# A two-layer transformer kernel: GpSimd's weight subtractions cut into 256-column pieces, and layer 0's gate operations spread over more places

## The chip, the cores and the metric

The kernel runs on one core of a Trainium2 chip. The metric is the device time of one execution in microseconds (us).

## What is computed

Input x has 4 batches of 1024 tokens with 128 features. Layer 0 adds to x a multi-query attention and a "SwitchHead" attention, both on the normalised x; layer 1 does the like with a linear attention and a mixture of experts. The change touches the SwitchHead part of layer 0 (8 heads, 8 experts each, 128 wide):

```python
raw = einsum('bsd,ed->bse', x, w).reshape(B, S, H, E)
probs = sigmoid(raw)
vals, idx = top_k(probs, 2)
vals = vals / clip(vals.sum(-1, keepdims=True), 1e-09) * route_scale
gate = (one_hot(idx, E) * vals[..., None]).sum(-2)      # for gate_v and for gate_o
xv = einsum('bsd,hedp->bshep', x, v_w)
v = einsum('bshep,bshe->bhsp', xv, gate_v)
att = softmax(einsum('bhqp,bhkp->bhqk', q, k) * SCALE)
ctx = einsum('bhqk,bhkp->bqhp', att, v)
out = einsum('bshep,hepd->bsd', ctx[:, :, :, None, :] * gate_o[..., None], o_w)
```

## The kernel before, in words

Layer 0 is the function `layer0`. It handles 32 steps (`N0`), one for each batch and SwitchHead head; in each step two heads of the multi-query attention are done beside it. Every engine has a block of its own in which one loop over `i` lists, by hand, what the engine does in which order; an engine does its list strictly in order, and semaphores join the lists. A tile is 128 tokens; there are 8 per batch. PSUM has a ring of five 512-column tiles, `ring`, and a two-bank tile, `wide`. TensorE takes the next ring tile with `claim`, which waits until the reader of the tile's last content is done. So a late VectorE operation that reads a ring tile holds up the matmuls five claims further on.

What matters of one step:

- **TensorE**: `values` (x times the value weights of 8 experts, 1024 columns per tile, as L79, L80 and L81), `peak_scores` (L254) and `scores_by_key` (L329) for the other attention, `scores` (into `wide`), `turn` (L295, transposes of the probabilities), `weigh` (L307), `outputs` (L79 to L81 with the output weights), `turn_peaks` (L274, needs L1139 of VectorE), `sum_by_key` (L344).
- **VectorE**: `take_peaks` (L1114) and `find_largest` (L1157) are maxima over PSUM tiles; `gate_values` (L1127) and `gate_outputs` (L1187) multiply a ring tile by the gates into `vprod` and `oprod`; `output_gates` (L1167 and L1169) works on small SBUF tiles; `cut_peaks` (L1137 to L1139), then `shift_queries` (L1146), which `scores` of tile 0 needs; `split_queries` (L65, L1106); `lower_ctx`. Between these stand eight calls `batch_work(i - 1, place)`, places 0 to 7.
- **GpSimd**: `sum_values` (L774 to L776) adds the experts' halves of `vprod` down to one tile of `vs`, `sum_outputs` (L783 to L787) those of `oprod` and adds them to x. Once per step it runs `lower_wv` and `lower_wo`.
- **ScalarE**: exponentials, copies out of PSUM, and the upper halves of the weights.

**Weight halves.** For precision each 32-bit operand is split in an upper part, rounded by the copy to the matmul's type, and a lower part, the difference. The weights of one head are 128 x 1024. They come by DMA into `wraw`, ScalarE copies the upper half (L826 and L834), and GpSimd's helper `lower` (L69) subtracts: one instruction of 1024 columns for the value weights (`m_wvs`), one for the output weights (`m_wos`). In GpSimd's order `lower_wv` stands between `sum_outputs` of tiles 3 and 4, and `lower_wo` between `sum_values` of tile 1 and of tile 2. TensorE's `values(i, 0, 0)` and the load of the next output weights wait for `wv_ready`; `outputs(n, 0, 0)` and the load of value weights wait for `wo_ready`.

**Batch work.** Per batch some work is left that belongs to no head: normalising, gates, keys, queries. VectorE does it for the batch after the current one in the `batch_work` calls; `s = i % 8` names the head of the batch, and `place` the call. The gates (`gates(b, part)`) are 16 parts for tiles 0 to 3 (q = 0) and the same 16 for tiles 4 to 7 (q = 1). One part is one link of a chain in which each operation waits for the one before (`gs` does that). Parts 0 to 12 find the two largest of 8 experts and take reciprocals. Part 13 is five operations on 64 or 128 columns (L1283 to L1287): the sum of the two inverses, the maximum with 1e-9, its reciprocal, the route scale, and the product. Part 14 (L1290, L1291) multiplies both choices by their shares, part 15 (L1293) adds them. Where the parts stand:

```python
                    if s == 1 and place >= 5:
                        gates(after, place - 5)
                    if s == 2 and place not in (0, 4):
                        gates(after, 2 + place - place // 4)
                    if s == 3 and place:
                        gates(after, 8 + place)
                    if s in (4, 5):
                        gates(after, 16 + 8 * (s - 4) + place)
```

So q = 0 ends in s = 3 (part 13 at place 5, part 14 at place 6, part 15 at place 7), and q = 1 in s = 5, at the same places; s = 4 has L1272 (part 6 of q = 1) at place 6. In s = 6 there are no gates. `lower_keys` (L1249) shares place 5 in s = 2 and s = 3, and `normalise` and `normalise_out` (L1214, L1225) stand at places 4 to 7 of s = 7 and s = 0. `choose_experts`, the routing of layer 1, ends with L1343; once it is called at s = 0, place 1. Place 1 lies between `cut_peaks` and `shift_queries`, place 5 before `gate_outputs` of tile 6, place 6 between the maxima of tile 3. For batch 0 all parts run in a row before the loop.

Of the kernel before, what the change touches and what calls it, by code (L numbers as in the profile page):

```python
# [31 lines left out]
def spread(ap, n):  # L32

    return ap.unsqueeze(len(ap.shape)).to_broadcast([*ap.shape, n])
# [33 lines left out]
def lower(eng, lo, src, hi):  # L68
    return eng.tensor_tensor(lo.bitcast(F32R), src, hi, ALU.subtract)  # L69
# [79 lines left out]
def layer0(nc, whole, a, x, xnT, ident, order, combine):  # L149
# [4 lines left out]
    with ExitStack() as ctx:  # L154
# [23 lines left out]
        wraw = m.sbuf("wraw", [D, ES * PS])  # L178
        wvs, wos = m.sbuf("wvs", [D, 2, ES * PS]), m.sbuf("wos", [PS, 2, ES * D])
# [20 lines left out]
        x_upper, wv_upper, wo_upper, x_ready, wv_ready, wo_ready, qk_upper, qk_ready, zeroed, zeros_stored, q_stored = m.sems(  # L200
            "x_upper wv_upper wo_upper x_ready wv_ready wo_ready qk_upper qk_ready zeroed zeros_stored q_stored")
# [23 lines left out]
        with nc.Block() as block:  # L225
# [483 lines left out]
            def _(pool):  # L709
# [46 lines left out]
                def lower_wv(n):  # L756
                    if n not in steps:
                        return
                    pool.wait_ge(wv_upper, n + 1)
                    lower(pool, wvs[:, 1, :], wraw[:, :], wvs[:, 0, :]).then_inc(wv_ready, 1)  # L760

                def lower_wo(n):
                    if n not in steps:
                        return
                    pool.wait_ge(wo_upper, n + 1)
                    lower(pool, wos[:, 1, :], wraw[:, :], wos[:, 0, :]).then_inc(wo_ready, 1)

                def sum_values(n, t):
                    if n not in steps:
# [326 lines left out]
            def _(v):  # L1096
# [155 lines left out]
                def gates(b, part):  # L1252
                    if b not in batches:
                        return
                    q, part = part // 16, part % 16
                    flat = gate_of[b % 2][:, 4 * q:4 * q + 4, :].rearrange("p t (g e) -> p (t g) e", e=ES)
                    ranks = order[:, :].unsqueeze(1).to_broadcast([P, 64, ES])
                    if part == 0:
                        v.wait_ge(gates_exp, 4 * b + 2 * q + 2)
                        gs(v.scalar_tensor_tensor(out=g_v[:, :, :], in0=flat, scalar=1.0, in1=flat, op0=ALU.add, op1=ALU.max))  # L1260
                    if part == 1:
                        gs(v.tensor_reduce(g_pair[:, 0, :], g_v[:, :, :], AX.X, ALU.min))
                    if part == 2:
                        gs(v.tensor_tensor(g_c[:, :, :], g_v[:, :, :], spread(g_pair[:, 0, :], ES), ALU.is_equal))
                    if part in (3, 9):
                        gs(v.tensor_tensor(g_c[:, :, :], g_c[:, :, :], ranks, ALU.mult))
                    if part in (4, 10):
                        gs(v.tensor_reduce(g_m[:, :], g_c[:, :, :], AX.X, ALU.max))
                    if part == 5:
                        gs(v.tensor_tensor(g_one[:, :, :], g_c[:, :, :], spread(g_m[:, :], ES), ALU.is_equal))  # L1270
                    if part == 6:
                        gs(v.scalar_tensor_tensor(out=g_v[:, :, :], in0=g_one[:, :, :], scalar=3.0e38, in1=g_v[:, :, :],  # L1272
                                                  op0=ALU.mult, op1=ALU.add))
                    if part == 7:
                        gs(v.tensor_reduce(g_pair[:, 1, :], g_v[:, :, :], AX.X, ALU.min))
                    if part == 8:
                        gs(v.tensor_tensor(g_c[:, :, :], g_v[:, :, :], spread(g_pair[:, 1, :], ES), ALU.is_equal))
                    if part == 11:
                        gs(v.tensor_tensor(g_other[:, :, :], g_c[:, :, :], spread(g_m[:, :], ES), ALU.is_equal))
                    if part == 12:  # L1280
                        gs(v.reciprocal(g_inv[:, :, :], g_pair[:, :, :]))
                    if part == 13:
                        gs(v.tensor_tensor(g_m[:, :], g_inv[:, 0, :], g_inv[:, 1, :], ALU.add))  # L1283
                        gs(v.tensor_tensor(g_m[:, :], g_m[:, :], tiny[:, :].to_broadcast([P, 64]), ALU.max))
                        gs(v.reciprocal(g_m[:, :], g_m[:, :]))
                        gs(v.tensor_tensor(g_m[:, :], g_m[:, :], route[:, :].to_broadcast([P, 64]), ALU.mult))
                        gs(v.tensor_tensor(g_inv[:, :, :], g_inv[:, :, :], g_m[:, :].unsqueeze(1).to_broadcast([P, 2, 64]),  # L1287
                                           ALU.mult))
                    if part == 14:
                        v.tensor_tensor(g_one[:, :, :], g_one[:, :, :], spread(g_inv[:, 0, :], ES), ALU.mult)  # L1290
                        gs(v.tensor_tensor(g_other[:, :, :], g_other[:, :, :], spread(g_inv[:, 1, :], ES), ALU.mult))  # L1291
                    if part == 15:
                        v.tensor_tensor(flat, g_one[:, :, :], g_other[:, :, :], ALU.add).then_inc(gates_ready, 1)  # L1293
                        v.wait_ge(gates_ready, 2 * b + q + 1)

# [59 lines left out]
                def batch_work(i, place):  # L1355
                    if i not in steps:
                        return
                    s, after, before, early = i % HS, i // HS + 1, i // HS - 1, i // HS - 2
                    if s in (1, 2) and place in (0, 4):
                        keep_v32(after, 2 * s - 2 + place // 4)  # L1360
                    if s in (2, 3) and place == 5:
                        lower_keys(after, s - 2)
                    if s == 0 and place == 2:
                        invert_dens(before)
                    if s == 4 and place in (0, 4):
                        add_attn(before, place // 4)
# [3 lines that stand above are left out]
                        gates(after, 2 + place - place // 4)  # L1370
                    if s == 3 and place:
                        gates(after, 8 + place)
                    if s in (4, 5):
                        gates(after, 16 + 8 * (s - 4) + place)
                    if s == 7 and place >= 4:
                        normalise(after + 1, (place - 4) // 2, place % 2)
                    if before == B - 2:
                        if s == 5 and place < 4:
                            token_moments(before, place)
                        if s == 5 and place == 4:  # L1380
                            statistics_out(before)
                        if s == 6 and place == 3:
                            rstd_out(before)
                        if s == 6 and place >= 4:
                            normalise_out(before, place // 6, place % 2)
                    elif s == 7 and place < 4:
                        token_moments(before, place)
                    if early < B - 2:
                        if s == 0 and place == 0:
                            statistics_out(early)  # L1390
                        if s == 0 and place == 5:
                            rstd_out(early)
                        if s == 0 and place >= 6:
                            normalise_out(early, 0, place % 2)
                        if s == 1 and place in (2, 3):
                            normalise_out(early, 1, place % 2)
                        if s == 3 and place == 4:
                            keep_routing(early)
                    if early == 1:
                        if s == 0 and place == 1:  # L1400
                            choose_experts(early - 1)
                        if s == 1 and place == 7:
                            mix(early - 1)
                        if s == 6 and place == 7:
                            choose_experts(early)
                        if s == 7 and place == 5:
                            mix(early)
# [18 lines left out]
                for q in range(2):  # L1426
                    normalise(1, q, 0)
                    normalise(1, q, 1)
                for part in range(32):
                    gates(0, part)  # L1430
                for i in range(-1, N0 + 1):
                    take_peaks(i, 5, 0, 1)
# [850 lines left out]
```

## Time and profile before

| what | value |
|---|---|
| median of 3 runs (lowest, highest) | 3594.96 us (3593.2, 3598.66) |
| the profiled execution: its own time, its span | 3593.13 us, 3591.4 us |
| mean granted TensorE clock | 0.967 |
| TensorE's matmuls busy | 3299.4 us (92%) |
| VectorE busy | 2363.4 us (66%) |
| GpSimd busy | 1755.3 us (49%) |
| the 32 + 32 subtractions (L69, 1024 columns) | 76.6 + 76.2 us, mean 2392 and 2382 ns |

The span runs from the first to the last instruction of the profiled execution; its own time is 1.7 us longer. In the names PE is TensorE, DVE VectorE, ACT ScalarE and POOL GpSimd. `m_wvs`, `m_wos` and so on are the tiles of the code with a prefix. A clock of 1.00 is 2.4 GHz, and 0.50 is 1.2 GHz.

### The profile page before, as it was taken

The page shows a single profiled execution, that of the slowest core. Times are in us where ns is not written, and L with a number is a line of the kernel's source. Part 1 is how long each engine was busy: PE and PEld are TensorE (multiplying, and loading weights), DVE is VectorE, ACT ScalarE, POOL GpSimd, SP SyncE. Part 2 cuts the span into 40 slices and gives each one's busy share as a digit, 9 for nine tenths or more (in the row PEclk, how much of TensorE's full clock was granted, in tenths as well). Part 3 has the DMA queues.
Part 4 walks back from the last instruction along what each step waited for, and adds up shares of the span by engine and source line. Part 5 has one row for each costly group of instructions (what it writes and reads, how often), then busy time and mean ns, then how long its engine had stood idle before and what let it go on. Part 6 is the DMA issues. An engine that isn't in the chain of part 4 may idle for free. (4 is left out here: it accounts for less than half of the span.)

```text
span 3591.4 us, 53232 instructions
## 1 busy us (share of the span) xinstructions
PE 3299.4 (92%) x19284; PEld 2311.3 (64%) x19284; DVE 2363.4 (66%) x3586; ACT 1687.0 (47%) x2854; POOL 1755.3 (49%) x1986
## 2 busy tenths in 40 slices
PE   3899999999999999999999999999993799989897
PEld 2566666666666666666666666666662677777675
DVE  6777888787888888888888888877863212122221
ACT  1445544545554445555454544555551363534444
POOL 1466656566665566666566665665652212121111
PEclk6999999999999999999999999999996899999998
DMA  3000000001000110010000001100003000000000
GB/s 86 18 25 26 19 19 28 28 26 31 20 19 19 30 33 25 20 32 19 24 29 28 19 20 32 31 19 19 25 2 67 9 1 1 1 1 1 1 1 24
DMA packets 115927, 79.23 MB, mean 22 GB/s; under 512 B 28618, under 2 KB 104020, under 8 KB 115668
## 3 DMA queue, kind: packets, MB, share of 16 engines
q1 hardware_dynamic: 113364, 73.46, 7.6%
q10 hardware_dynamic: 2304, 2.36, 0.3%
q8 instruction: 157, 2.57, 0.3%
q14 instruction: 102, 0.84, 0.1%
HBM read 63.74 MB, written 12.06 MB: 21 GB/s over the span
## 5 line engine op out<-in xcount | busy, mean ns | idle before, releaser
L883 ACT ACTIVATE m_expA<-m_ring 128x512 f32<-128x512 f32 x1024 | 547.5, 602 | 420.5 <-PE m_ring L329 297.4
L1114 DVE TENSOR_REDUCE m_peaks<-m_ring 128x1 f32<-128x512 f32 x1024 | 653.0, 684 | 126.1 <-PE m_ring L254 119.0
L774 POOL TENSOR_TENSOR m_vprod<-m_vprod 128x512 f32<-128x512 f32 x256 | 333.5, 1303 | 622.0 <-DVE m_vprod L1127 620.7
L783 POOL TENSOR_TENSOR m_oprod<-m_oprod 128x512 f32<-128x512 f32 x256 | 327.8, 1280 | 328.5 <-DVE m_oprod L1187 328.2
L307 PE MATMUL m_ring<-m_probT,m_vs 128*128 128x256 f32 x2048 | 466.8, 381 | 1.7 <-ACT m_probT L864 1.7
L864 ACT ACTIVATE m_probT<-m_ring 128x512 f32<-128x512 f32 x512 | 284.3, 601 | 363.5 <-PE m_ring L295 333.8
L307 PEld LDWEIGHTS m_ring<-m_probT,m_vs 128*128 128x128 f32 x2048 | 391.2, 191 | 60.3 <-ACT m_probT L864 2.2
L1127 DVE TENSOR_TENSOR m_vprod<-m_ring,m_gate 128x512 f32<-128x512 f32 x512 | 341.4, 687 | 77.7 <-POOL m_vs L776 55.0
L1157 DVE TENSOR_REDUCE m_neg<-m_wide 128x1 f32<-128x1024 f32 x256 | 312.7, 1221 | 105.7 <-PE m_wide L81 105.4
L1187 DVE TENSOR_TENSOR m_oprod<-m_ring,m_go 128x512 f32<-128x512 f32 x512 | 347.0, 688 | 31.0 <-PE m_ring L81 16.5
L2161 POOL TENSOR_TENSOR k_x<-k_x,m_mixed 128x512 f32<-128x512 f32 x72 | 91.9, 1276 | 534.5 <-DVE m_mixed L1970 534.5
L2080 ACT ACTIVATE m_hT<-m_ring,l_b 128x512 f32<-128x512 f32 x288 | 182.7, 686 | 352.5 <-PE m_ring L81 352.3
L1970 DVE TENSOR_TENSOR m_mixed<-m_ring,k_combine 128x512 f32<-128x512 f32 x72 | 49.8, 692 | 450.7 <-PE m_ring L1810 450.7
L854 ACT ACTIVATE m_prob<-m_wide,m_neg 128x1024 f32<-128x1024 f32 x256 | 288.3, 1126 | 104.3 <-DVE m_neg L1157 104.3
L295 PE MATMUL m_ring<-k_ident,m_prob 128*128 128x128 f32 x2048 | 275.9, 277 | 26.9 <-DVE m_peaks L1114 26.1
L295 PEld LDWEIGHTS m_ring<-k_ident,m_prob 128*128 128x128 f32 x2048 | 233.0, 142 | 92.8 <-issue 66.3
L1810 PEld LDWEIGHTS m_ring<-l_w,m_hT 128*128 128x128 f32 x2304 | 273.6, 195 | 8.9 <-issue 2.7
L344 PE MATMUL m_sums<-m_expA,m_v 128*32 128x512 f32 x2048 | 275.1, 609 | 1.5 <-ACT m_expA L883 1.4
L1810 PE MATMUL m_ring<-l_w,m_hT 128*128 128x128 f32 x2304 | 274.2, 278 | 1.1 <-ACT m_qpT L2060 1.1
L79 PE MATMUL m_ring<-m_wvs,m_xs 128*128 128x512 f32 x512 | 237.2, 463 | 35.1 <-DVE m_oprod L1187 23.6
L254 PE MATMUL m_ring<-m_ks,m_qs 32*128 32x512 f32 x1024 | 229.4, 504 | 33.4 <-DVE m_qs L1106 28.5
L79 PE MATMUL m_wide<-m_xs,m_yT 128*128 128x512 f32 x512 | 231.0, 451 | 9.2 <-DVE m_qs L1146 5.7
(249 smaller groups left out, 6239.5 us busy)
## 6 DMA issues: line engine op xcount, KB each, us to landing
m_wraw<-in_v_w SPq DMA_DIRECT2D x32, 512.0 KB, 4.0
m_qf<-q_dram SPq DMA_DIRECT2D x128, 128.0 KB, 2.7
m_wraw<-in_o_w SPq DMA_DIRECT2D x32, 512.0 KB, 3.8
q_dram<-m_kf SPq DMA_DIRECT2D x24, 256.0 KB, 4.3
sums_dram<-m_sumsT ACTq DMA_DIRECT2D x128, 18.0 KB
m_o_in<-sums_dram SPq DMA_DIRECT2D x64, 32.0 KB
m_rden_in<-rden_dram SPq DMA_DIRECT2D x64, 32.0 KB
p_w<-in_w SPq DMA_DIRECT2D x1, 2048.0 KB, 8.3
```

Source lines behind the costliest of these rows:

```text
L79: pe.matmul(out, wh, xh, start=True, stop=False)
L295: last = pe.transpose(ps[:, c * P:(c + 1) * P], prob[t % 2][:, (4 * h + c) * P:(4 * h + c + 1) * P], ident[:, :])
L307: last = pe.matmul(ps[:, 0:2 * P], vs[n % 2][:, k, :], probT[g % 2][:, k, :], start=(k == 0), stop=(k == TPB - 1))
L774: vchain(pool.tensor_tensor(vprod[:, 0:512], vprod[:, 0:512], vprod[:, 512:1024], ALU.add))
L783: ochain(pool.tensor_tensor(op[:, 0:512], op[:, 0:512], op[:, 512:1024], ALU.add))
L854: act.activation(prob[t % 2][:, :], wide.home["scores", n, t][:, :], ACT.Exp, bias=neg[t % 2][:, :], accum_out=den[n % 2][:, t:t + 1]).the ...
L883: act.activation(expA[hh][:, c * 512:(c + 1) * 512], ring.home["scT", n, k, hh, c][:, :], ACT.Exp)\
L1114: v.tensor_reduce(peaks[:, t, hh, c:c + 1], ring.home["peaks", n, t, hh, c][:, :], AX.X, ALU.max)\
L1127: v.tensor_tensor(vprod[:, c * 512:(c + 1) * 512].rearrange("p (e d) -> p e d", e=4), ring.home["values", n, t, c][:, :].rearrange("p (e d ...
L1157: v.tensor_reduce(neg[t % 2][:, :], wide.home["scores", n, t][:, :], AX.X, ALU.max, negate=True)\
L1187: v.tensor_tensor(oprod[t % 2][:, c * 512:(c + 1) * 512].rearrange("p (e d) -> p e d", e=4), ring.home["outputs", n, t, c][:, :].rearrange ...
L1810: last = pe.matmul(ps[:, t * P:(t + 1) * P], hT[j % 2][:, k, t * P:(t + 1) * P], w2[:, e, k, :], start=(k == 0), stop=(k == HT - 1))
```

## The change

GpSimd's two subtractions per step become four instructions of 256 columns each; the semaphore is raised by the last. The five operations of part 13 become four parts (13: the sum; 14: the maximum; 15: reciprocal and route scale; 16: the product), so that q = 0 and q = 1 have 19 parts each, 38 together; six of them now stand in s = 6. In s = 3 places 5, 6 and 7 hold parts 13, 14 and 15; s = 4 begins with parts 16, 17, 18 of q = 0 and goes on with parts 0 to 4 of q = 1; s = 5 has parts 5 to 12 of q = 1, and s = 6 has parts 13 to 18 at places 0 to 5.

```diff
--- before.py
+++ after.py
@@ -757,13 +757,17 @@
                     if n not in steps:
                         return
                     pool.wait_ge(wv_upper, n + 1)
-                    lower(pool, wvs[:, 1, :], wraw[:, :], wvs[:, 0, :]).then_inc(wv_ready, 1)
+                    for cols in (slice(256 * k, 256 * (k + 1)) for k in range(4)):
+                        last = lower(pool, wvs[:, 1, cols], wraw[:, cols], wvs[:, 0, cols])
+                    last.then_inc(wv_ready, 1)
 
                 def lower_wo(n):
                     if n not in steps:
                         return
                     pool.wait_ge(wo_upper, n + 1)
-                    lower(pool, wos[:, 1, :], wraw[:, :], wos[:, 0, :]).then_inc(wo_ready, 1)
+                    for cols in (slice(256 * k, 256 * (k + 1)) for k in range(4)):
+                        last = lower(pool, wos[:, 1, cols], wraw[:, cols], wos[:, 0, cols])
+                    last.then_inc(wo_ready, 1)
 
                 def sum_values(n, t):
                     if n not in steps:
@@ -1252,7 +1256,7 @@
                 def gates(b, part):
                     if b not in batches:
                         return
-                    q, part = part // 16, part % 16
+                    q, part = part // 19, part % 19
                     flat = gate_of[b % 2][:, 4 * q:4 * q + 4, :].rearrange("p t (g e) -> p (t g) e", e=ES)
                     ranks = order[:, :].unsqueeze(1).to_broadcast([P, 64, ES])
                     if part == 0:
@@ -1281,15 +1285,18 @@
                         gs(v.reciprocal(g_inv[:, :, :], g_pair[:, :, :]))
                     if part == 13:
                         gs(v.tensor_tensor(g_m[:, :], g_inv[:, 0, :], g_inv[:, 1, :], ALU.add))
+                    if part == 14:
                         gs(v.tensor_tensor(g_m[:, :], g_m[:, :], tiny[:, :].to_broadcast([P, 64]), ALU.max))
+                    if part == 15:
                         gs(v.reciprocal(g_m[:, :], g_m[:, :]))
                         gs(v.tensor_tensor(g_m[:, :], g_m[:, :], route[:, :].to_broadcast([P, 64]), ALU.mult))
+                    if part == 16:
                         gs(v.tensor_tensor(g_inv[:, :, :], g_inv[:, :, :], g_m[:, :].unsqueeze(1).to_broadcast([P, 2, 64]),
                                            ALU.mult))
-                    if part == 14:
+                    if part == 17:
                         v.tensor_tensor(g_one[:, :, :], g_one[:, :, :], spread(g_inv[:, 0, :], ES), ALU.mult)
                         gs(v.tensor_tensor(g_other[:, :, :], g_other[:, :, :], spread(g_inv[:, 1, :], ES), ALU.mult))
-                    if part == 15:
+                    if part == 18:
                         v.tensor_tensor(flat, g_one[:, :, :], g_other[:, :, :], ALU.add).then_inc(gates_ready, 1)
                         v.wait_ge(gates_ready, 2 * b + q + 1)
 
@@ -1370,7 +1377,7 @@
                         gates(after, 2 + place - place // 4)
                     if s == 3 and place:
                         gates(after, 8 + place)
-                    if s in (4, 5):
+                    if s in (4, 5) or s == 6 and place < 6:
                         gates(after, 16 + 8 * (s - 4) + place)
                     if s == 7 and place >= 4:
                         normalise(after + 1, (place - 4) // 2, place % 2)
@@ -1426,7 +1433,7 @@
                 for q in range(2):
                     normalise(1, q, 0)
                     normalise(1, q, 1)
-                for part in range(32):
+                for part in range(38):
                     gates(0, part)
                 for i in range(-1, N0 + 1):
                     take_peaks(i, 5, 0, 1)
```

The order of instructions shows the moves. First VectorE in s = 3 around place 5, before: L1187 is `gate_outputs`, L1249 `lower_keys`, `m_g_...` are the gates' tiles.

```order
L1187 TENSOR_TENSOR m_oprod<-m_ring,m_go 128x512
L1249 SCALAR_TENSOR_TENSOR m_ks<-m_ks,m_split,m_kf 128x512
L1283 TENSOR_TENSOR m_g_m<-m_g_inv 128x64
L1284 TENSOR_TENSOR m_g_m<-m_g_m,m_tiny 128x64
L1285 RECIPROCAL m_g_m<-m_g_m 128x64
L1286 TENSOR_TENSOR m_g_m<-m_g_m,m_route 128x64
L1287 TENSOR_TENSOR m_g_inv<-m_g_inv,m_g_m 128x128
L1187 TENSOR_TENSOR m_oprod<-m_ring,m_go 128x512
L1157 TENSOR_REDUCE m_neg<-m_wide 128x1
```

And with the change (line numbers are four higher up to the sum of the inverses, L1287, and up to seven higher behind it):

```order
L1191 TENSOR_TENSOR m_oprod<-m_ring,m_go 128x512
L1253 SCALAR_TENSOR_TENSOR m_ks<-m_ks,m_split,m_kf 128x512
L1287 TENSOR_TENSOR m_g_m<-m_g_inv 128x64
L1191 TENSOR_TENSOR m_oprod<-m_ring,m_go 128x512
L1161 TENSOR_REDUCE m_neg<-m_wide 128x1
L1131 TENSOR_TENSOR m_vprod<-m_ring,m_gate 128x512 x2
```

Four operations have left the place between L1249 and the next `gate_outputs`. Then VectorE in s = 3, places 6 and 7, before:

```order
L1114 TENSOR_REDUCE m_peaks<-m_ring 128x1 x3
L1290 TENSOR_TENSOR m_g_one<-m_g_one,m_g_inv 128x512
L1291 TENSOR_TENSOR m_g_other<-m_g_other,m_g_inv 128x512
L1114 TENSOR_REDUCE m_peaks<-m_ring 128x1
L1127 TENSOR_TENSOR m_vprod<-m_ring,m_gate 128x512 x2
L1157 TENSOR_REDUCE m_neg<-m_wide 128x1
L1293 TENSOR_TENSOR m_gate<-m_g_one,m_g_other 128x512
L1127 TENSOR_TENSOR m_vprod<-m_ring,m_gate 128x512
```

And with the change:

```order
L1118 TENSOR_REDUCE m_peaks<-m_ring 128x1 x3
L1289 TENSOR_TENSOR m_g_m<-m_g_m,m_tiny 128x64
L1118 TENSOR_REDUCE m_peaks<-m_ring 128x1
L1131 TENSOR_TENSOR m_vprod<-m_ring,m_gate 128x512 x2
L1161 TENSOR_REDUCE m_neg<-m_wide 128x1
L1291 RECIPROCAL m_g_m<-m_g_m 128x64
L1292 TENSOR_TENSOR m_g_m<-m_g_m,m_route 128x64
L1131 TENSOR_TENSOR m_vprod<-m_ring,m_gate 128x512
```

The two products of 512 columns have left place 6, which now holds one operation on 64 columns; place 7 holds a reciprocal and a product on 64 columns in place of the last addition. The products now stand in s = 4, at place 1. Last, GpSimd around the output weights, before:

```order
L774 TENSOR_TENSOR m_vprod<-m_vprod 128x512
L775 TENSOR_TENSOR m_vprod<-m_vprod 128x256
L776 TENSOR_TENSOR m_vs<-m_vprod 128x128
L69 TENSOR_TENSOR m_wos<-m_wraw,m_wos 128x1024
L774 TENSOR_TENSOR m_vprod<-m_vprod 128x512
```

And with the change:

```order
L778 TENSOR_TENSOR m_vprod<-m_vprod 128x512
L779 TENSOR_TENSOR m_vprod<-m_vprod 128x256
L780 TENSOR_TENSOR m_vs<-m_vprod 128x128
L69 TENSOR_TENSOR m_wos<-m_wraw,m_wos 128x256 x4
L778 TENSOR_TENSOR m_vprod<-m_vprod 128x512
```

Nothing has moved against its neighbours there; the one subtraction is now four in a row.

## Rows read from the trace of the kernel before

**Rows 1.** The page, part 1: busy us, share of the span, instructions of each engine.

```profile
PE 3299.4 (92%) x19284; PEld 2311.3 (64%) x19284; DVE 2363.4 (66%) x3586; ACT 1687.0 (47%) x2854; POOL 1755.3 (49%) x1986
```

**Rows 2.** TensorE's waits, 100 to 2640 us: us in total, times, longest.

```profile
PE m_ring L295 <- DVE m_peaks L1114: 26.1, 13, 2.5
PE m_ring L79 <- DVE m_oprod L1187: 23.6, 13, 4.3
...
PE m_wide L79 <- DVE m_qs L1146: 5.7, 1, 5.7
```

**Rows 3.** Windows: length; PE, PEld, DVE, ACT, POOL busy (x); PEclk; DMA share; GB/s.

```profile
1004.47:1086.91 82.44, 80.82 (x426) 54.47 (x425) 68.00 (x101) 41.50 (x75) 52.88 (x61) 1.00 0.07 21
1086.91:1177.82 90.91, 82.76 (x426) 55.02 (x425) 74.57 (x105) 42.18 (x75) 49.86 (x60) 0.94 0.07 19
...
1261.37:1343.90 82.53, 78.07 (x410) 52.41 (x409) 67.34 (x100) 40.17 (x73) 49.77 (x59) 0.98 0.10 30
...
2484.44:2562.79 78.35, 77.61 (x416) 52.22 (x415) 63.59 (x99) 39.74 (x72) 48.83 (x59) 1.00 0.08 22
```

**Rows 4.** Timeline of TensorE, phases 3, 3, 4, 5 and 7: start, us, operation [idle before].

```profile
1105.01 0.76 PE L79 MATMUL m_ring<-m_wvs,m_xs 128*128 128x512 f32 x1 [4.26 <-DVE m_oprod L1187]
...
1132.83 1.06 PE L295 MATMUL m_ring<-k_ident,m_prob 128*128 128x128 f32 x8 [2.45 <-DVE m_peaks L1114]
...
1217.88 1.06 PE L295 MATMUL m_ring<-k_ident,m_prob 128*128 128x128 f32 x8 [1.84 <-DVE m_peaks L1114]
...
1275.46 0.47 PE L79 MATMUL m_ring<-m_wvs,m_xs 128*128 128x512 f32 x1 [1.79 <-DVE m_oprod L1187]
...
1461.04 1.06 PE L295 MATMUL m_ring<-k_ident,m_prob 128*128 128x128 f32 x8 [1.51 <-DVE m_peaks L1114]
```

**Rows 5.** Timeline of VectorE, same columns, single operations.

```profile
58.84 0.23 DVE L1284 TENSOR_TENSOR m_g_m<-m_g_m,m_tiny 128x64 f32<-128x64 f32 x1
...
1017.06 0.88 DVE L1249 SCALAR_TENSOR_TENSOR m_ks<-m_ks,m_split,m_kf 128x512 fp32r<-128x512 f32 x1
...
1087.00 2.30 DVE L1169 TENSOR_TENSOR m_go<-m_gate,m_rden 128x16 f32<-128x16 f32 x1
...
1099.42 1.30 DVE L1283 TENSOR_TENSOR m_g_m<-m_g_inv 128x64 f32<-128x64 f32 x1
...
1103.30 0.83 DVE L1287 TENSOR_TENSOR m_g_inv<-m_g_inv,m_g_m 128x128 f32<-128x128 f32 x1
...
1128.96 2.40 DVE L1290 TENSOR_TENSOR m_g_one<-m_g_one,m_g_inv 128x512 f32<-128x512 f32 x1
...
1214.62 2.38 DVE L1272 SCALAR_TENSOR_TENSOR m_g_v<-m_g_one,m_g_v 128x512 f32<-128x512 f32 x1
...
1425.07 0.60 DVE L1214 TENSOR_SCALAR m_xn<-k_x,m_mean,m_rstd 128x128 f32<-128x128 f32 x2
...
1458.12 2.17 DVE L1214 TENSOR_SCALAR m_xn<-k_x,m_mean,m_rstd 128x128 f32<-128x128 f32 x2
...
2159.43 2.31 DVE L1343 TENSOR_TENSOR m_lg<-m_lg,m_t_first 128x64 f32<-128x64 f32 x1
```

**Rows 6.** Timeline of GpSimd, single operations.

```profile
1016.93 0.46 POOL L787 TENSOR_TENSOR k_x<-k_x,m_oprod 128x128 f32<-128x128 f32 x1
...
1017.36 1.72 POOL L774 TENSOR_TENSOR m_vprod<-m_vprod 128x512 f32<-128x512 f32 x1
...
1022.07 0.73 POOL L784 TENSOR_TENSOR m_oprod<-m_oprod 128x256 f32<-128x256 f32 x1
...
1023.83 1.28 POOL L774 TENSOR_TENSOR m_vprod<-m_vprod 128x512 f32<-128x512 f32 x1
...
1128.43 2.38 POOL L69 TENSOR_TENSOR m_wos<-m_wraw,m_wos 128x1024 fp32r<-128x1024 f32 x1
```

**Rows 7.** Timeline of VectorE in a head without batch work.

```profile
2602.95 0.69 DVE L1127 TENSOR_TENSOR m_vprod<-m_ring,m_gate 128x512 f32<-128x512 f32 x1 [1.68 <-POOL m_vs L776]
...
2605.18 0.42 DVE L69 TENSOR_TENSOR m_ctxT<-m_ring,m_ctxT 128x256 fp32r<-128x256 f32 x1 [1.07 <-ACT m_ctxT L874]
```

## Prediction, made before the changed kernel ran

> **What bounds the kernel now.** Start with the busy shares: TensorE works 92% of the span, VectorE 66%, GpSimd 49% [rows 1]. So only what makes TensorE stand, or slows its clock, can change the time. Next, TensorE's waits from 100 to 2640 us, which is layer 0 without its ends: the first two lines, with VectorE as the releaser, make 50 us, and one single wait for L1146 5.7 us [rows 2]. Then the windows, cut where GpSimd starts the subtraction for the value weights of one head after another [rows 3]. "Phase s" is from here on the batch work's number at that start; its places 3 to 7 lie in the window, and places 0 to 2 of the next phase at its end. The last row is a head without batch work: 78.35 us, TensorE busy 77.61. Phases 2, 3 and 5 take 82.44, 90.91 and 82.53. Phase 3 records as many matmuls as phase 2 (426) and is 8.5 us longer: idle time grows from 1.62 to 8.15 us, and busy time from 80.82 to 82.76, with the granted clock at 0.94 instead of 1.00. The timeline of TensorE shows where the idle time sits [rows 4]: 4.26 and 2.45 us in phase 3, 1.84 in phase 4, 1.79 in phase 5 (and a second 2.45 there), 1.51 in phase 7. The pattern stands three times, once for each later batch; the 1.51 kind stands at four heads.
>
> VectorE's timeline names the causes [rows 5]. The 4.26 us wait ends behind five small gate operations, the first at 1099.42, the last ended at 1104.13. The waits before L295 end behind L1290 and L1291, L1272, or two L1214. L1290 takes 2.40, L1272 2.38, the two L1214 2.17 together, though the same two take 0.60 elsewhere. Set GpSimd beside it [rows 6]: its subtraction for the output weights starts at 1128.43 and takes 2.38 us; L1290 starts 0.53 us later and ends 0.55 us after it. So a VectorE operation with two SBUF sources, and L1214 with one, doesn't get through before the GpSimd instruction then under way has ended.
>
> **The gates' operations in four places.** In phase 3, place 5, four of the five leave. From the end of the first (1100.72) to the end of the last (1104.13) that is 3.41 us, all in front of the L1187 that frees a ring tile for TensorE: 4.26 falls to 0.85. In phase 5 place 5 holds one 512-wide reduction instead (about 0.6 us, near the 0.55 that L1290 needs once it runs), and 1.79 falls to 0. Nobody but VectorE's own queue waits for these operations: the gates are read a batch later.
>
> The later parts move back three places, in the second half of a batch six. Place 6 gets: in phase 3 one 64-wide operation (0.23 us, from the uncontended row of L1284) for L1290 and L1291; in phase 4 the product with the ranks for L1272; in phase 5 L1279 for L1290 and L1291. New are two products at place 1 of phase 4, ahead of L1146, and six parts in phase 6, which had none. Between turning the peaks and the scores that need L1146 TensorE has the values of tile 7 and a transpose, and in phase 4 a projection and the queries too. So the products may cost nothing; at most 4.8, if each lasts as L1290 does. I take 0.5, nearer the cover. Phase 6 gets the five operations (4.7 us at phase 3's contended durations) and three 512-wide ones (1.8): at most 6.5, at least 0. They stand one or two to a place, where the other phases hold as much and TensorE shows no wait over 1 us, so I take 1.0.
>
> **The subtractions in pieces.** A 256-column GpSimd operation takes 0.73 us, a 512-column one 1.28 [rows 6]. Four pieces are 2.92 us against 2.38: 0.54 us more for each of 64 subtractions, 35 us of GpSimd's time. Who waits for that? For the value weights nobody soon: their reader stands half a head later in TensorE's order. Behind the output weights stands the sum of tile 2's values, for which VectorE waits 1.68 us in a head without batch work; and then, two small operations later, 1.07 us for ScalarE [rows 7]. A sum that is 0.54 us late disappears in that 1.07, so I price it at nothing; were that cover gone, it would be 0.54 x 32 = 17 us.
> The Trainium skill, page "GPSIMD Engine Reference", section "Elementwise — side-by-side cycle accounting", gives a two-input operation about 2.6 cycles an element at 1.2 GHz, and no price for one instruction more. By that alone four pieces last as long as one whole; the rows disagree, with 0.73 for 256 columns where half of 1.28 is 0.64, and the sum goes by the rows.
>
> What a piece gives: an operation that starts 0.53 us into the subtraction waits until the first piece ends, 0.2 us instead of 1.85. How much of VectorE's delay at place 6 reaches TensorE can be read off: L1272 2.4 us of delay, 1.84 of wait; L1290 with L1291 3.0 and 2.45; two L1214 2.1 and 1.51. The cover is 0.6 us each time. So at place 6:
> - phase 3: delay 0.2 + 0.23, the wait of 2.45 goes to 0
> - phases 4 and 5: 0.2 + 0.6, the waits of 1.84 and 2.45 go to 0.2
> - normalising (four heads): 0.2 + 0.3, then the second L1214 meets the second piece, 0.73 + 0.3; together 1.5, and 1.51 goes to 0.9.
> At the value weights L1169 takes 2.30 us at worst and should stay under 0.9; VectorE idles soon after, so I book nothing. In the head with the 5.7 us wait the routing's last operation, L1343, is 2.31 us of it; with pieces about 0.9, so 1.4 saved.
>
> Does the port change hands between two pieces? One place bears on it: L1249 starts at 1017.06, inside L787; L787 ends at 1017.39; the next GpSimd operation, listed from 1017.36 with no wait, takes 1.72 us instead of 1.28, as if it had begun when L1249 ended [rows 5, 6]. VectorE got in between two adjacent GpSimd instructions. I take that as how it goes.
>
> **The sum.** Per batch, three times: phase 3 saves 3.41 + 2.45, and 1.94 by the clock (82.76 - 80.82): 7.8. Phase 4 saves 1.6. Phase 5 saves 1.79 + 2.2 and 1.0 by the clock (0.98 over 82.53 us is 3.3 us at the lower level, 1.6 lost, of which I take two thirds): 5.0. That is 14.4 x 3 = 43.2. Normalising 0.6 x 4 = 2.4; routing 1.4, and 0.5 for the clock. Together 47.5. Against it phase 6 with 1.0 x 3, phase 4's products 0.5 x 3, and 2 for small new waits: 6.5. Net 41. From the profiled execution's 3593.1 us that is 3552; the median of the runs shown is 1.8 us higher, so 3554.
>
> **Rivals.**
> B. GpSimd keeps the port through its four adjacent pieces, since they wait for nothing. For it: each piece is ready when the last ends. Against it: the place of L1249. Then the pieces change only the length. Phase 3 keeps 3.4, 0.5 and 1.2 of clock; phase 4 loses 0.6; phase 5 keeps 1.8 and 0.6 of clock: 6.9 x 3 = 20.7, less 0.5 x 5 for normalising and routing and the 6.5. About 12 saved: 3583.
> The Trainium skill, page "SBUF — State Buffer", section "SBUF: two separate sides", calls the pair of ports that VectorE shares with GpSimd an exclusive lock, held for the whole instruction by whoever starts first; by that rule a queued piece could start first each time. On "whole instruction" the trace agrees (L1290 ends 0.55 us after the 2.38 us subtraction); on who is next it has the place of L1249.
> C. The waits go, but a part comes back: VectorE loses the pauses in which it caught up, and ring tiles are freed late elsewhere. For it: TensorE idles 0.74 us even in a head without batch work, so it is never far ahead or behind. With a third of the 47.5 returning 25 us are saved: 3570.
> D. Slower. Short GpSimd instructions cost more here than in the chains, and the sum of tile 2 is late in every head. It decides from the point where the subtraction's excess uses up the 1.07 and the 0.6 of cover, at pieces of (2.38 + 1.67) / 4 = 1.01 us. At 1.28 each, the 512-column duration, the excess is 2.74 - 1.67 = 1.07 us x 32 = 34 us, and such pieces give back most of place 6; with 12 us kept, 3617. Against it: 0.73 for that width.
>
> **How the numbers follow.** Forecast 0.70 (3543 to 3566), B 0.13, C 0.12, D 0.03, and 0.02 for gains and new waits that cancel. A measurement of this kernel tells 0.2%, some 7 us, from no change. All but D and the last are faster by more: 0.95, 0.02, 0.03. The likeliest gives 3554. The range goes up through C to 3575 and down to 3543, where the work added to phases 4 and 6 costs nothing and every clock loss goes.
>
> **What would show it.** Pieces near 0.73 us; in phase 3 the new place 6 (the maximum with the small constant) under 0.5 us; a wait near 0.9 where 4.26 stood, without a lower clock behind it; waits before the probability transposes under 1 us; phase 3 near 83 us, phase 5 near 79. Wrong would be: two-source operations that still last over 2 us inside a subtraction (B), VectorE waiting over 2.7 us for the sum of tile 2 (D), or new waits of over 1 us in phases 4 and 6 (C).

## The result, and the profile after

| | before | changed |
|---|---|---|
| median of 6 runs (lowest, highest) | 3596.41 us (3593.2, 3599.15) | 3539.9 us (3537.73, 3541.45) |
| ratio to before, 95% interval | | 0.9842 (0.983 to 0.9855) |
| span of the profiled execution | 3591.4 us | 3537.4 us |

The changed kernel is 56.5 us faster, 1.6%; the spans differ by 54.0 us. The forecast was 41 us and 3554; the time lies 3 us under the range. The direction and the places are right, several sizes are not. In the experiments below one run each of choice and both took 9654.92 and 4143.19 us, for which nothing here gives a cause, and the ratios leave these two out.

The list of TensorE's waits from 100 to 2640 us of the changed kernel (us in total, times, longest), against [rows 2]:

```profile
PE m_ring L79 <- DVE m_oprod L1191: 7.9, 10, 1.3
PE m_wide L79 <- DVE m_qs L1150: 4.1, 1, 4.1
...
PE m_ring L295 <- DVE m_peaks L1118: 2.6, 10, 0.4
```

The waits before L295 fell from 26.1 to 2.6 us, those of L79 for `gate_outputs` from 23.6 to 7.9. Together that is 39 us. The rest is mostly busy time. From the second window's start to the last one's, before and changed:

```profile
118.28:2562.79 2444.51, 2371.94 (x12576) 1595.87 (x12576) 1985.04 (x2968) 1222.95 (x2209) 1490.28 (x1740) 0.99 0.09 25
...
119.12:2510.42 2391.30, 2359.30 (x12575) 1589.47 (x12575) 1949.47 (x2968) 1219.32 (x2209) 1524.40 (x1919) 1.00 0.09 25
```

TensorE's idle time there falls from 72.6 to 32.0 us, and its busy time by 12.6 for the same matmuls, while the mean granted clock rises from 0.99 to 1.00. The windows by step, cut as before (length; busy us of PE, PEld, DVE, ACT, POOL; granted clock), phases 2, 3, 5 and 6, and the head with the long routing:

```profile
986.38:1068.86 82.48, 80.84 (x426) 54.49 (x425) 68.53 (x101) 41.41 (x75) 53.65 (x67) 1.00 0.07 21
1068.86:1148.63 79.77, 78.68 (x426) 53.09 (x425) 67.82 (x102) 41.87 (x75) 51.86 (x65) 1.00 0.08 22
...
1230.73:1308.33 77.60, 76.92 (x412) 51.45 (x411) 64.90 (x101) 40.33 (x73) 51.12 (x65) 1.00 0.11 32
1308.33:1387.21 78.88, 77.85 (x416) 52.49 (x415) 65.11 (x102) 39.65 (x72) 50.61 (x64) 1.00 0.08 22
...
2108.93:2195.32 86.39, 83.05 (x426) 56.38 (x427) 68.73 (x108) 43.28 (x77) 49.68 (x64) 0.96 0.14 33
```

Phase 2 is unchanged. Phase 3 fell from 90.91 to 79.77 [rows 3]; its idle time from 8.15 to 1.09, and its busy time from 82.76 to 78.68. That is lower than phase 2's 80.84 at the same count of matmuls and the same clock: the two windows hold different matmuls. Phase 5 fell from 82.53 to 77.60.

The timelines of the changed kernel, one row of TensorE, two of VectorE, and GpSimd's four pieces, show why:

```profile
1082.56 0.47 PE L79 MATMUL m_ring<-m_wvs,m_xs 128*128 128x512 f32 x1 [0.83 <-DVE m_oprod L1191]
```

```profile
1080.39 1.30 DVE L1287 TENSOR_TENSOR m_g_m<-m_g_inv 128x64 f32<-128x64 f32 x1
...
1104.48 0.27 DVE L1289 TENSOR_TENSOR m_g_m<-m_g_m,m_tiny 128x64 f32<-128x64 f32 x1
```

```profile
1103.94 2.81 POOL L69 TENSOR_TENSOR m_wos<-m_wraw,m_wos 128x256 fp32r<-128x256 f32 x4
```

Place 5 of phase 3 holds one gate operation, and TensorE waits 0.83 us where it waited 4.26; 0.85 was forecast. At place 6 L1289 starts 0.54 us into the first piece and lasts 0.27, so it got through at the border of the first and the second piece: seen one by one, the first piece ends at 1104.68 and the second starts at 1104.63 (the two records overlap by 0.05 us). The four pieces take 2.81 us (2.92 was forecast). A 512-column operation gets in too, but then the pieces pay for it; place 6 of phase 4:

```profile
1185.57 0.73 DVE L1270 TENSOR_TENSOR m_g_c<-m_g_c,k_order 128x512 f32<-128x512 f32 x1
...
1185.01 3.25 POOL L69 TENSOR_TENSOR m_wos<-m_wraw,m_wos 128x256 fp32r<-128x256 f32 x4
```

The second piece lasts 1.18 us there, the others 0.72 to 0.74.

### The profile page after: what moved, and what is told of

Its sections match the earlier page's. It is cut to its first block and busy times, and to the rows that moved or that the text cites. A ratio compares the mean times of both kernels' runs of the same rounds, so it can differ in the third digit from the quotient of the medians.

```text
span 3537.4 us, 53430 instructions
## 1 busy us (share of the span) xinstructions
PE 3290.1 (93%) x19284; PEld 2306.5 (65%) x19284; DVE 2327.5 (66%) x3586; ACT 1682.4 (48%) x2854; POOL 1790.7 (51%) x2178
## 5 line engine op out<-in xcount | busy, mean ns | idle before, releaser
L295 PE MATMUL m_ring<-k_ident,m_prob 128*128 128x128 f32 x2048 | 273.6, 275 | 3.3 <-DVE m_peaks L1118 2.6
L295 PEld LDWEIGHTS m_ring<-k_ident,m_prob 128*128 128x128 f32 x2048 | 231.7, 141 | 68.4 <-issue 42.1
L79 PE MATMUL m_ring<-m_wvs,m_xs 128*128 128x512 f32 x512 | 235.0, 459 | 19.4 <-POOL m_wvs L69 11.3
L79 PE MATMUL m_wide<-m_xs,m_yT 128*128 128x512 f32 x512 | 231.3, 452 | 7.6 <-DVE m_qs L1150 4.1
```

Source lines behind the costliest of these rows:

```text
L79: pe.matmul(out, wh, xh, start=True, stop=False)
L295: last = pe.transpose(ps[:, c * P:(c + 1) * P], prob[t % 2][:, (4 * h + c) * P:(4 * h + c + 1) * P], ident[:, :])
```

## Experiments

All are timed in up to five rounds beside the kernel before, which had a median of 3593.19 us beside the first four kernels (pieces_only to wv_pieces), 3597.65 beside halves, eighths, wo_twice and slots, and 3594.87 beside the last four.

**The two halves of the change.** The kernel pieces_only is the kernel before with this edit, and the same one for `wvs` and `wv_ready`:

```diff
-lower(pool, wos[:, 1, :], wraw[:, :], wos[:, 0, :]).then_inc(wo_ready, 1)
+for cols in (slice(256 * k, 256 * (k + 1)) for k in range(4)):
+    last = lower(pool, wos[:, 1, cols], wraw[:, cols], wos[:, 0, cols])
+last.then_inc(wo_ready, 1)
```

The kernel gates_only is the changed kernel with both subtractions whole, this edit undone.

> Pieces as in the change, gates as before. Theory (VectorE gets the port at the end of each 256-column piece): the waits before L295 shrink in phases 3, 4 and 5 and where normalising stands at place 6, the 4.26 and 1.79 us waits at place 5 stay. Idle saved per batch 2.1 + 1.6 + 2.1, plus 1.2 x 4 and 1.6 for the routing, plus some 3 us per batch by the clock: about 33 us under the kernel before, 3563. Rival (GpSimd keeps the port through adjacent pieces): nothing gained, some 3 us lost by the longer subtraction, 3599.

> Gates as in the change, subtractions whole. Theory: place 5 of phases 3 and 5 is cleared (3.4 and 1.8 us), the operation at place 6 still starts 0.53 us into a 2.38 us subtraction and lasts 2.1 to 2.5 us, so TensorE still waits 1.5 to 2 us before L295; the clock stays up behind place 5. About 32 us under the kernel before, 3564. If instead the gates' places alone made the whole gain, it is 3540.

Measured: pieces_only 3568.03 us, 0.993 (0.9917 to 0.9942), 25 us saved; gates_only 3562.68 us, 0.9915 (0.9902 to 0.9929), 30.5 us saved. The pieces alone were expected to save 33 us, the gates 32. The sum, 55.7, is the whole change: the parts hardly overlap. Phase 3 in pieces_only, with the two longest waits that are left in it:

```profile
1076.76:1163.72 86.96, 80.74 (x425) 53.81 (x425) 71.94 (x105) 42.01 (x75) 52.24 (x66) 0.96 0.07 20
```

```profile
1093.87 0.77 PE L79 MATMUL m_ring<-m_wvs,m_xs 128*128 128x512 f32 x1 [4.25 <-DVE m_oprod L1191]
...
1120.40 1.06 PE L295 MATMUL m_ring<-k_ident,m_prob 128*128 128x128 f32 x8 [1.31 <-DVE m_peaks L1118]
```

And in gates_only, with the wait at place 6 of phase 3 and that of phase 5:

```profile
1076.93:1159.24 82.31, 79.05 (x426) 53.09 (x425) 71.01 (x102) 42.12 (x75) 50.51 (x60) 1.00 0.07 21
```

```profile
1116.31 1.06 PE L295 MATMUL m_ring<-k_ident,m_prob 128*128 128x128 f32 x8 [1.38 <-DVE m_peaks L1114]
...
1281.19 1.06 PE L295 MATMUL m_ring<-k_ident,m_prob 128*128 128x128 f32 x8 [1.82 <-DVE m_peaks L1114]
```

```profile
1113.52 1.92 DVE L1285 TENSOR_TENSOR m_g_m<-m_g_m,m_tiny 128x64 f32<-128x64 f32 x1
```

Two things follow. Rival B is out: with old gates the pieces alone gain 25 us, and a 64-wide operation that lasts 1.92 us inside a whole subtraction lasts 0.27 inside a cut one. And the clock: phase 3 is busy 82.76 us with both long waits, 80.74 with only that of 4.25, 79.05 with only waits of 1.4 and less, 78.68 with none over 0.9. So in this batch each of the two long waits costs some 2 us more at the lower level behind it, 4.1 in all. In the phases 3 of the other two batches the same two steps, from the kernel before to pieces_only and on to the changed kernel, are 2.6 and 1.4 us, and 0.6 and 2.0. A long wait need not cost anything: the third phase 5 of the kernel before has waits of 1.78 and 2.42 us at a clock of 1.00, and the wait of 1.82 us in phase 5 of gates_only leaves the clock of its window at 1.00:

```profile
1242.80:1322.55 79.75, 76.81 (x410) 51.22 (x408) 67.48 (x99) 40.12 (x73) 49.39 (x60) 1.00 0.10 31
```

**Which of the two subtractions counts.** The changed kernel with one of them whole: wo_pieces has this edit, wv_pieces the same for `wos` and `wo_ready`.

```diff
-for cols in (slice(256 * k, 256 * (k + 1)) for k in range(4)):
-    last = lower(pool, wvs[:, 1, cols], wraw[:, cols], wvs[:, 0, cols])
-last.then_inc(wv_ready, 1)
+lower(pool, wvs[:, 1, :], wraw[:, :], wvs[:, 0, :]).then_inc(wv_ready, 1)
```

> The change, but the value weights' subtraction whole. Theory: only the subtraction for the output weights meets operations that TensorE waits for; within 3 us of the changed kernel, 3540 to 3543, with the routing's 1.6 us back and the 0.8 us of the start gone. Rival (VectorE's L1169 at the value weights matters in every head): 10 us or more slower than the changed kernel.

> The change, but the output weights' subtraction whole. Theory: like the kernel with the gates alone, less 1.6 us for the routing: 3562. Rival (the value weights matter): near 3550.

Measured: wo_pieces 3546.22 us, 0.9871 (0.9856 to 0.9886); wv_pieces 3560.09 us, 0.9905 (0.9891 to 0.9919). The output weights carry most of what the pieces bring. The median of wo_pieces is higher than the expected 3540 to 3543. Its interval just misses the changed kernel's (0.983 to 0.9855) and overlaps that of change_again below (0.9834 to 0.9861); by the ratios it is 8 to 10 us slower than the changed kernel. Its profiled run was the fastest of its four, with a span of 3538.5 us. There its windows differ from the changed kernel's by 0.9 us in one phase 3, 0.5 in each phase 5 and 0.6 at the routing, 3 us in all, and wv_pieces is 2.6 us faster than gates_only. So the windows give the value weights' pieces about 3 us; what the slower median adds to that stays open.

**How small a piece must be.** Two pieces of 512 columns in halves, the first edit in both loops, and eight of 128 in eighths, the second.

```diff
-for cols in (slice(256 * k, 256 * (k + 1)) for k in range(4)):
+for cols in (slice(512 * k, 512 * (k + 1)) for k in range(2)):
...
-for cols in (slice(256 * k, 256 * (k + 1)) for k in range(4)):
+for cols in (slice(128 * k, 128 * (k + 1)) for k in range(8)):
```

> The change with two pieces of 512 columns. Theory (the wait is the rest of the GpSimd instruction under way, of which 0.6 us is covered): the operation at place 6 starts 0.53 us into a piece of 1.28 and waits 0.75 instead of 0.2; TensorE's waits before L295 become 0.4 in phase 3 and 0.75 in phases 4 and 5 and where normalising stands there. That is about 6 us over the changed kernel, 3546. If any cut were enough, or the port stayed with GpSimd, it would be equal to the changed kernel or 20 us and more above it.

> The change with eight pieces of 128 columns, 0.46 us each by L776: 3.5 us for a subtraction instead of 2.8, 1.1 more than before the change. Theory: place 6 now meets the second piece and waits 0.3 us, which the cover of 0.6 takes; the sum of tile 2 is late by less than the 1.67 us of cover. Within 4 us of the changed kernel, 3540 to 3544. If the lengthening counted without cover, 32 x 0.7 = 22 us more, 3562.

Measured: halves 3549.82 us, 0.9868 (0.9854 to 0.9881), eighths 3540.02 us, 0.9837 (0.9823 to 0.985). In halves, place 6 of phase 4:

```profile
1192.35 1.06 PE L295 MATMUL m_ring<-k_ident,m_prob 128*128 128x128 f32 x8 [0.76 <-DVE m_peaks L1118]
```

Expected was 0.75. Where normalising stands at place 6 the wait is 1.36 to 1.40, not 0.8: the second L1218 meets the second half. That, four times, is 2.5 us of the 3.8 by which halves came out above the expected 3546. Eighths equal the changed kernel although GpSimd works 3.38 us on each subtraction, 1.0 more than before the change. VectorE's wait for the sum of tile 2 tells where that went, in a head without batch work of eighths:

```profile
2551.02 0.69 DVE L1131 TENSOR_TENSOR m_vprod<-m_ring,m_gate 128x512 f32<-128x512 f32 x1 [2.49 <-POOL m_vs L780]
```

2.49 us here, 1.95 in the changed kernel, 1.68 before [rows 7]; and the last window, a head without batch work, takes 78.4 us in all three.

**The price when the cover is used up.** The output weights' pieces run twice, the second time after the first has ended (`ochain` waits for that).

```diff
 for cols in (slice(256 * k, 256 * (k + 1)) for k in range(4)):
     last = lower(pool, wos[:, 1, cols], wraw[:, cols], wos[:, 0, cols])
+ochain(last)
+for cols in (slice(256 * k, 256 * (k + 1)) for k in range(4)):
+    last = lower(pool, wos[:, 1, cols], wraw[:, cols], wos[:, 0, cols])
 last.then_inc(wo_ready, 1)
```

> The change with the output weights' four pieces run twice over (same values): the sum of tile 2 is 3.2 us later than before the change instead of 0.4. Theory: 1.07 and 0.6 us of that are covered, the rest, 1.5 us, reaches TensorE in each of 32 heads: 50 us, and more where waits lower the clock; 3590 or above. If the cover is larger than I read, less; without any, 32 x 2.8 = 90 us, 3630.

Measured: 3626.77 us, 1.0085 (1.0069 to 1.0101). Two heads without batch work, both with the same new wait of 1.76 us; in the first the clock fell too, and a second wait, of 0.56 us, came with it:

```profile
2342.03:2425.97 83.94, 81.40 (x432) 55.12 (x430) 61.51 (x92) 39.65 (x72) 54.86 (x71) 0.98 0.07 21
2425.97:2507.18 81.21, 79.45 (x432) 54.01 (x431) 61.29 (x94) 39.65 (x72) 52.37 (x69) 1.00 0.07 21
```

```profile
2470.10 0.47 PE L79 MATMUL m_ring<-m_wos,m_ctxT 128*128 128x512 f32 x1 [1.76 <-DVE m_vprod L1134]
```

```profile
2550.47 0.69 DVE L1134 TENSOR_TENSOR m_vprod<-m_ring,m_gate 128x512 f32<-128x512 f32 x1 [4.80 <-POOL m_vs L783]
```

The sum of tile 2 is 4.80 - 1.68 = 3.1 us later than before the change, 1.76 of it reach TensorE: 1.4 us are covered, where I had read 1.07 + 0.6. In all 31 waits of this kind, of 1.27 to 1.94 us, take 54.4 us from 100 to 2640 us, near the 50 expected. The kernel is slower than the changed one by more, 87 us by the ratios; to the last window's start it has 21 us more busy time, with a clock of 0.98 in ten windows that the changed kernel passes at 1.00. That the time is also near the 3630 expected without any cover is chance, since the waits show the cover. Rival D's mechanism exists, with this price; 256-column pieces stay clear of it.

**Can more be had from the gates' places?** First, parts 13 and 14, and 15 and 16, share a place, and place 5 of phases 2 and 3, where `lower_keys` stands, stays free of gates.

```diff
+free = [(1, 5), (1, 6), (1, 7), (2, 1), (2, 2), (2, 3), (2, 6), (2, 7), (3, 1), (3, 2), (3, 3), (3, 4),
+        (3, 6), (3, 7)] + [(s, place) for s in (4, 5, 6) for place in range(8)]
+groups = [[19 * q + p for p in g] for q in range(2)
+          for g in [[p] for p in range(13)] + [[13, 14], [15, 16], [17], [18]]]
+gate_slots = dict(zip(free, groups))
...
-if s == 1 and place >= 5:
-    gates(after, place - 5)
-if s == 2 and place not in (0, 4):
-    gates(after, 2 + place - place // 4)
-if s == 3 and place:
-    gates(after, 8 + place)
-if s in (4, 5) or s == 6 and place < 6:
-    gates(after, 16 + 8 * (s - 4) + place)
+for part in gate_slots.get((s, place), ()):
+    gates(after, part)
```

> The change with the gates' parts laid out anew: parts 13 and 14, and 15 and 16, share a place, so that place 5 of phases 2 and 3, where the keys' lower half stands, holds no gate operation. Theory: the waits of 1.30 (phase 2) and 0.83 us (phase 3) before L79 go, the reciprocal of 0.95 us comes to place 6 of phase 3 and costs 0.5: 1.5 us per batch, 4 to 5 us under the changed kernel, 3535. Rival (a place's load is only moved, the wait turns up elsewhere): equal to the changed kernel.

Measured: 3544.38 us, 0.9857 (0.9844 to 0.9871). The rival holds. The waits at place 5 are gone (phase 2 82.03 instead of 82.48), but at the end of phase 5's window a new one stands, ahead of the scores of tile 0, because reciprocal, product and product now lie before L1150; phases 3 and 6 are 0.5 and 1.2 us longer.

```profile
1313.21 0.47 PE L79 MATMUL m_wide<-m_xs,m_yT 128*128 128x512 f32 x1 [1.49 <-DVE m_qs L1150]
```

Then keys_late moves the keys alone, to the place where VectorE waits for GpSimd anyway:

```diff
-if s in (2, 3) and place == 5:
+if s in (2, 3) and place == 7:
     lower_keys(after, s - 2)
```

In choice the thirteen routing operations of `choose_experts` are cut over four places, 3, 3, 3 and 4 of them in order in the new `choose_part`, and ScalarE's exponentials follow later. The kernel both has the two edits, and change_again is the changed kernel once more.

```diff
-if s == 0 and place == 1:
-    choose_experts(early - 1)
+if s == 0 and place in (1, 2, 3, 4):
+    choose_part(early - 1, place - 1)
...
-if s == 0 and place == 0 and early == 1:
+if s == 1 and place == 1 and early == 1:
     routing_exps(early - 1)
```

> The change, with the keys' lower half at place 7 instead of place 5 in phases 2 and 3. At place 7 VectorE waits 0.6 us and more for GpSimd's sum of tile 2, so it is covered there. Theory: the wait of 1.30 us in phase 2 falls to 0.3, the one of 0.83 in phase 3 to 0, nothing comes back: 1.8 us per batch, 5 us under the changed kernel. Rival (as in the new layout of the slots, the load comes back at another place): no gain.

> The change, with the thirteen routing operations that stand at one place (head 26) cut over places 1 to 4, and ScalarE's exponential for them one head later. Theory: the wait of 4.13 us for L1150 falls to under 1 and the clock (0.96 in that window) stays up: 3 + 2 us, 5 us under the changed kernel. Rival: the operations hold up the maxima over the scores instead, and the scores of tile 1 are late: no gain.

> Both edits: if they are independent, 10 us under the changed kernel.

> The changed kernel itself, as the yardstick for the three others on the same chip: 0.984 of the kernel before, and how far a second profile of the same program differs window by window.

| kernel | median us | ratio to before, 95% |
|---|---|---|
| keys_late | 3534.26 | 0.983 (0.9817 to 0.9843) |
| choice | 3537.45 | 0.9833 (0.982 to 0.9847) |
| both | 3532.45 | 0.9817 (0.9804 to 0.9831) |
| change_again | 3542.3 | 0.9848 (0.9834 to 0.9861) |

The intervals of keys_late and choice overlap that of change_again, and that of both just misses it; the windows are clearer. Phases 2 and 3 of keys_late, and the window with the long routing (head 26) of choice:

```profile
985.35:1066.87 81.52, 80.89 (x426) 54.49 (x425) 67.86 (x101) 41.31 (x75) 53.65 (x67) 1.00 0.07 21
1066.87:1145.65 78.78, 78.53 (x426) 53.06 (x425) 66.66 (x102) 41.75 (x75) 51.72 (x65) 1.00 0.08 22
```

```profile
2109.64:2190.62 80.98, 79.33 (x423) 53.25 (x422) 67.74 (x111) 43.17 (x77) 49.69 (x64) 1.00 0.15 35
```

The keys give 1.0 us in each of six windows (82.48 to 81.52, 79.77 to 78.78), with no new wait, as expected. The cut routing gives 5.4 us against the changed kernel's 86.39, or 4.1 against its second profile (85.08). Both together is the fastest kernel of this study by its median, 10 us under the changed kernel on the same chip, which is what independent edits were expected to give.

## Why the prediction was right or wrong

Right was what bounds the kernel, and both mechanisms. In the spans, from the start of the first window to the last and behind it:

| term | forecast | measured |
|---|---|---|
| phase 3, three times | -23.4 | -30.2 |
| phase 4, with its products at place 1 | -3.3 | -4.7 |
| phase 5 | -15.0 | -14.8 |
| normalising and routing (phases 7 and 0) | -4.3 | -5.5 |
| phase 6 | +3.0 | +1.7 |
| small waits elsewhere | +2.0 | +1.1 |
| behind the last window | 0 | -1.6 |
| sum | -41 | -54.0 |

The step that failed is the clock's term in phase 3, "1.94 by the clock (82.76 - 80.82)". It took phase 2's busy time for what phase 3 would have at full clock, because both record 426 matmuls, and took one batch for all three. Equal counts were not equal work: at full clock phase 3 is busy 78.68 us. The three phases 3 lost 3.95, 4.08 and 2.61 us of busy time to the clock, 10.6 and not 5.8. The windows are cut by GpSimd's order and not by TensorE's. So in this batch phase 2 of the kernel before holds 71 of the matmuls of `weigh` and phase 3 holds 59 (first two lines below), and phase 3 makes up the count with 16 short ones. In the first of the three batches both hold 64, and there the same comparison (last two lines) gives 3.92 us, close to the 3.95 measured.

```profile
L307 PE MATMUL m_ring<-m_probT,m_vs 128*128 128x256 f32 x71 | 16.1, 379 | 0.0
...
L307 PE MATMUL m_ring<-m_probT,m_vs 128*128 128x256 f32 x59 | 14.6, 403 | 0.0
...
349.78:430.37 80.59, 78.93 (x418) 52.87 (x417) 66.76 (x99) 41.51 (x75) 50.47 (x58) 1.00 0.08 21
430.37:520.83 90.46, 82.85 (x418) 54.82 (x417) 73.43 (x105) 42.07 (x75) 49.84 (x58) 0.94 0.07 19
```

The third batch gives 2.33 that way. The row at hand also set a bound above 1.94: a mean clock of 0.94 over 90.91 us is 10.9 us at the lower level and at most 5.5 lost, and for phase 5 I had used just that reading.

The other terms:

- The other part of that phase, 3.41 + 2.45 us of waits, was right: 0.85 was forecast for the place-5 wait and 0.83 measured, and 0 at place 6. Idle time in the three phases fell by 19.6 us where these two terms give 17.6.
- Place 6 of phases 4 and 5: 0.2 us of wait forecast, 0.20 measured. The cover of 0.6 us holds.
- Normalising: a wait of 0.9 forecast, 0.35 measured. I let the second L1218 wait for the second piece and then take 0.3 us; the pair lasted 1.01, not 1.5 us.
- The costs, 6.5 us, were booked too high. The products at place 1 of phase 4 show no new wait, phase 6 costs 0.6 us each time, and VectorE's lost pauses show nowhere. Most of that sum was caution and not a row.
- The lengthened subtraction, priced at nothing, costs nothing that shows, as eighths confirms.
- The sign "phase 5 near 79" doesn't follow from the prediction's own sum: 82.53 less 5.0 is 77.5, and 77.60 was measured.
- B and D fell, B by pieces_only, D by eighths and wo_twice. C too: nothing of the gain came back.

So the clock accounts for 4.8 of the 13 us between 41 and 54, the other costs and normalising for about 5, idle time in phase 3 that I had not listed for 2, and the part behind layer 0's last window for 1.6. That last part also varies by itself, as below.

The Trainium skill's lock for the whole instruction ("SBUF — State Buffer", section "SBUF: two separate sides") is borne out for the single instruction (L1290 ends 0.55 us behind the subtraction of 2.38 us it fell into, L1285 of gates_only lasts 1.92 us). Its "whoever starts first" doesn't mean that adjacent GpSimd instructions keep the ports: behind the start of the changed kernel no two-source VectorE operation that begins during the four pieces lasts over 1.28 us, where up to 2.40 stood before. The rate of the page "GPSIMD Engine Reference" (section "Elementwise — side-by-side cycle accounting") in the Trainium skill, taken alone, would have four pieces last as long as one whole. They last 2.81 us against 2.38.

## What to carry to other kernels

A long GpSimd instruction over SBUF stalls a two-source VectorE operation that falls into it until it ends, even one of 64 columns (1.92 us here against 0.27); cut it so that the rest of a piece stays under the cover of the engine that is waited for, and check who stands behind the lengthened work. Small chained operations of one engine belong spread over its order, best where it waits for another engine anyway; moving them elsewhere at random only moves the wait. When pricing a clock drop, bound it by the window's own time at half clock, and compare with a neighbour only where it holds the same kinds of matmuls and not just as many; look at every batch and not at one.

## What the runs showed that was not expected

- The border of a GpSimd instruction is enough. L1289 (64 columns) starts 0.54 us into a piece, ends at 1104.75, and the four pieces still take 2.81 us, 0.70 from one start to the next. A short VectorE operation slips between two pieces at no cost that shows; a 512-column one makes the four 3.25 us long.
- The same program spends different time outside the steady part. The window behind the start took 73.3 us at a clock of 1.00 in the first profile of the changed kernel and 77.0 at 0.96 in the second, and what follows the last window 1027.0 and 1029.9 us. The windows between agree within 0.1 us, except one phase 4 (82.13 and 81.95) and the routing's (86.39 and 85.08). A few us between two spans of this kernel say nothing; windows tell effects of 0.5 us.
- The same wait of 1.76 us in wo_twice came once with a clock of 0.98 and once with 1.00, 2 us of busy time apart. A recurring wait under 2 us can therefore cost about twice its length in some heads; what decides in which stays open.
